# Rounding the sigmoids on GpSimd in the largest-output pass, and the key biases' product on 128 rows in the masked attention

## The chip, the cores and the metric

One core of a Trainium2 chip runs the whole program. The core has five engines that each work through their own list of instructions in order and wait for each other on semaphores: TensorE (matrix products, PE), VectorE (DVE), ScalarE (ACT), GpSimd (POOL) and SyncE (SP), which here only starts transfers. The metric is the device time of one execution in microseconds; lower is better. A profile is one more execution with every instruction recorded.

## The reference

Two decoder layers on x of shape (16, 256, 512): a cross attention, a quantized feed-forward network, a masked attention and a second feed-forward network with mixed low-rank parts, each added to x. The change touches two stages. The first is in the quantized network:

```python
up   = act_qdq(x @ lpbq_dequant(w_up).T)
gate = act_qdq(x @ lpbq_dequant(w_gate).T)
sig  = fixed_qdq_u16(jax.nn.sigmoid(gate))   # clip(round(sig * 65536), 0, 65535) / 65536
gate = act_qdq(gate * sig)
o    = act_qdq(gate * up)                    # its scale needs max |gate * up| over everything
return o @ lpbq_dequant(w_down).T
```

Since `act_qdq` divides by the largest magnitude of the whole tensor, the products have to be gone through once for the maximum before any of them can be used. The second is the masked attention:

```python
qp, kp = _proj(q, W1, b1, W2, b2), _proj(k, W1, b1, W2, b2)
qk   = einsum('bqd,bkd->bqk', qp, kp) / sqrt(512) + mask
return einsum('bqk,bkd->bqd', softmax(qk), v1)
```

The kernel folds both projections into the keys, so that a score is a product of normalized x with a folded key, plus one number for each key, the key bias.

## The kernel before

The stages run one after the other. **The largest-output pass** (`output_maximum`, names `om_`) cuts the 4096 x 1536 gates into 48 parts of 128x1024 that stay in SBUF as integers (`qf_gate`). Two parts make a pair. For an even part n the sigmoids are made here: ScalarE computes them into `sig` (L1614), VectorE rounds them to uint16 in `sq[:, 0, :]` (L1703); for an odd part they come rounded from HBM (`sq_d`, L1579), where the pass before left them. Then for each part: VectorE multiplies gate by sigmoid (`prod`, L1713), ScalarE scales the raw up-product (L1621, loaded by SP at L1582) and the product (L1623, back into `qf_gate`), VectorE multiplies both (`outp`, L1725) and reduces the magnitudes to a maximum (L1729). VectorE's order is written out: ahead of an even part's output product it rounds the sigmoids of the part after the next, n + 2; after each output product comes the sigmoid product of part n + 2, and then the reduction. `sig` is a single buffer, so the next sigmoid waits for `sq_done`; the next rounding waits for `prod_done`, since `sq[:, 0]` is single too.

Beside that pass, the keys of the masked attention are folded. TensorE turns the weights, multiplies them and forms a Gram matrix; from part 16 on it multiplies the Gram matrix with the context, eight chunks of 512 keys in four row blocks each, and forms the key biases. For that, half-chunks of the context are loaded by GpSimd (L1760, one buffer, so each load waits until TensorE has turned the last one), turned by TensorE (L1798) and split into a high part by ScalarE (L1632) and a low part by VectorE (L1718, one operand in PSUM). GpSimd also does the small tasks of the fold: it sets two tiles, loads context half 1, adds and spreads the key shift (L1770, L1772), splits the four Gram rows (L1775, L1777), forms and splits the shift's parts (L1779 to L1784), and then starts the other 14 context loads, in this order and each as soon as its wait is met. At the end it reduces the maximum over the partitions (L1788).

**The masked attention** (`masked_attention`, names `ma_`) goes through 16 batches of 256 tokens in a software pipeline. In step s TensorE turns x of batch s + 1 (L2256), forms the scores of batch s, turns the probabilities of s - 1 (L2281) and multiplies those of s - 2 with the values. The scores of each of two query tiles begin with the key biases: `ones[:]` of 2 rows times `trow[:, b, :]`, 2 rows by 256 keys (a high and a low part of the bias), at L2269, start=True; twelve products of 128 rows with 256 columns follow in the same PSUM tile (L190 to L192 in `product`). `trow` is loaded by SP (L2075) from `split_d` in HBM. GpSimd's list begins with a memset of `ones` (L2109), then come the deviations (L2097, L2099) and the low parts of keys and values (L2103, L2107).

Of the kernel before, what the change touches and what calls it, by code (L numbers as in the profile page):

```python
# [14 lines left out]
ALU = mybir.AluOpType  # L15
# [8 lines left out]
P = 128  # L24
# [1470 lines left out]
def output_maximum(nc, a, ctx_in, keys_d, bias_d, raw_up, gate, sq_d, big, scal, folds, wd, wd_parts, wd_late, ident):  # L1495
# [9 lines left out]
    with Phase(nc, "om") as ph:  # L1505
# [7 lines left out]
        mx_row = ph.sb("mx_row", [P, 1])  # L1513
        raw_ready = [ph.sem(f"raw_ready{i}") for i in range(2)]
        sq_ready = [ph.sem(f"sq_ready{i}") for i in range(2)]
        sig_ready, sq_done = ph.sem("sig_ready"), ph.sem("sq_done")
        up_ready, prod_done, gate_ready, out_done, max_done = (
            ph.sem(n) for n in ("up_ready", "prod_done", "gate_ready", "out_done", "max_done"))
        spacer = ph.sem("spacer")
# [46 lines left out]
        with nc.Block() as block:  # L1566
# [129 lines left out]

            @block.vector
            def _(dve):
                def rounded(n):
                    dve.wait_ge(sig_ready, n // 2 + 1)  # L1700
                    if n >= 2:
                        dve.wait_ge(prod_done, n - 1)
                    dve.tensor_scalar(sq[:, 0, :], sig[:], SIGQ, SIGQ - 1, ALU.mult, ALU.min).then_inc(sq_done, 1)  # L1703

                def products(n):
                    s = n % 2
                    if s:
                        dve.wait_ge(sq_ready[n // 2 % 2], 16 * (n // 4) + 16)
                    else:
                        dve.wait_ge(sq_done, n // 2 + 1)  # L1710
                    if n >= 2:
                        dve.wait_ge(gate_ready, n - 1)
                    dve.tensor_tensor(prod[:, s, :], place(n), sq[:, place_of(n), :], ALU.mult).then_inc(prod_done, 1)  # L1713

                def context_low(x):
                    c, lo = x // 2, x % 2 * S
                    dve.wait_ge(c_hi, x + 1)
                    dve.tensor_tensor(cT[c % 2][:, 1, :, lo:lo + S], ctp[:], cT[c % 2][:, 0, :, lo:lo + S].bitcast(F32), ALU.subtract).then_inc(c_low, 1)  # L1718

                def outputs(n):  # L1720
                    dve.wait_ge(gate_ready, n + 1)
                    dve.wait_ge(up_ready, n + 1)
                    if n:
                        dve.wait_ge(max_done, n)
                    dve.tensor_tensor(outp[:], place(n), up[:, n % 2, :], ALU.mult).then_inc(out_done, 1)  # L1725

                def largest(n):
                    dve.wait_ge(out_done, n + 1)
                    dve.tensor_reduce(mx[:, n:n + 1], outp[:], AX_X, ALU.max, apply_absolute_value=True).then_inc(max_done, 1)  # L1729

                rounded(0)
                products(0)
                products(1)
                for n in range(N):
                    if n % 2 == 0 and n + 2 < N:
                        rounded(n + 2)
                    outputs(n)
                    if n + 2 < N:
                        products(n + 2)
                    if n == 10:  # L1740
                        context_low(0)
                    if n == 15:
                        context_low(1)
# [12 lines left out]
            def _(pool):  # L1756
                def load_context(x):
                    if x:
                        pool.wait_ge(c_full, x)
                    pool.dma_start(cin[:], ctx_in[x * S:(x + 1) * S, :].rearrange("(t p) d -> p t d", p=P)).then_inc(c_ready, 16)  # L1760
# [3 lines left out]
                pool.wait_ge(cleared, 1)  # L1764
                pool.memset(gbraw, 1.0).then_inc(cleared, 1)
                pool.wait_ge(cleared, 2)
                load_context(1)
                pool.wait_ge(b_ready, 32)
                pool.wait_ge(beta_out, 1)
                pool.tensor_tensor(beta[:], bsum[:], b12[:, 1, :], ALU.add).then_inc(beta_ready, 1)  # L1770
                pool.wait_ge(beta_ready, 1)
                pool.tensor_tensor(betas, betas, beta[:].unsqueeze(2).broadcast_to([P, KD, P]), ALU.mult).then_inc(betas_ready, 1)  # L1772
                for d in range(KD):
                    pool.wait_ge(g_out, d + 1)
                    pool.tensor_copy(gram[:, 0, d, :], graw[:, d, :]).then_inc(gram_hi, 1)  # L1775
                    pool.wait_ge(gram_hi, d + 1)
                    pool.tensor_tensor(gram[:, 1, d, :], graw[:, d, :], gram[:, 0, d, :].bitcast(F32), ALU.subtract).then_inc(gram_low, 1)  # L1777
                pool.wait_ge(gc_out, 2)
                pool.tensor_tensor(gbraw, gbraw, gcol[:].unsqueeze(2).broadcast_to([P, KD, P]), ALU.mult).then_inc(gbraw_done, 1)  # L1779
                pool.wait_ge(gbraw_done, 1)  # L1780
                pool.wait_ge(turned, KD)
                pool.tensor_copy(gb[:, 0], gbraw).then_inc(gb_hi, 1)
                pool.wait_ge(gb_hi, 1)
                pool.tensor_tensor(gb[:, 1], gbraw, gb[:, 0].bitcast(F32), ALU.subtract).then_inc(gb_low, 1)  # L1784
                for x in range(2, 2 * NCH):
                    load_context(x)
                pool.wait_ge(row_max, 1)
                pool.partition_all_reduce(big[:, 0:1], mx_row[:], P, RMAX).then_inc(all_max, 1)  # L1788

# [195 lines left out]
def masked_attention(nc, a, ctx_in, keys_d, bias_d, split_d, x2, x3, sides, ident, neghalf):  # L1985
# [8 lines left out]
    with Phase(nc, "ma") as ph:  # L1994
# [13 lines left out]
        mask = ph.sb("mask", [P, NK, S])  # L2008
        traw = ph.sb("traw", [B, S])
        tsplit = ph.sb("tsplit", [B, 2, S], F32R)  # L2010
        trow = ph.sb("trow", [2, B, S], F32R)
        ones = ph.sb("ones", [2, P], F32R)
        logit = ph.sb("logit", [P, 2, NK, S])
        nm = ph.sb("nm", [P, 2, NK])
        prob = ph.sb("prob", [P, 2, NK, S])
# [7 lines left out]
        po = ph.ps("po", [P, NK, D])  # L2023
        x_ready, stored = ([ph.sem(f"{n}{i}") for i in range(NX)] for n in ("x_ready", "stored"))
        r_ready, c_ready = [ph.sem(f"r_ready{i}") for i in range(NR)], [ph.sem(f"c_ready{i}") for i in range(NC)]
        m_ready, traw_ready, t_high, t_low, t_stored, t_ready, ones_made = (
            ph.sem(n) for n in ("m_ready", "traw_ready", "t_high", "t_low", "t_stored", "t_ready", "ones_made"))
        stat_done, mv_ready, var_ready, rstd_ready, shift_ready, xn_ready, spacer_d, spacer_p, spacer_a = (
            ph.sem(n) for n in ("stat_done", "mv_ready", "var_ready", "rstd_ready", "shift_ready", "xn_ready", "spacer_d", "spacer_p", "spacer_a"))
        x_full, x_high, x_low, r_high, r_low, v_high, v_low = (  # L2030
# [10 lines left out]
        def _(sp):  # L2041
# [30 lines left out]
            load_keys(2)  # L2072
            load_x(3)
            sp.wait_ge(t_stored, 16)
            sp.dma_start(trow[:].bitcast(F32), split_d.rearrange("b a s -> a b s")).then_inc(t_ready, 16)  # L2075
            for s in range(LAST + 1):
                if s + 3 < B:
                    load_keys(s + 3)
# [13 lines left out]
        def _(pool):  # L2092
# [12 lines left out]
            def values_low(b):  # L2105
                pool.wait_ge(v_high, b + 1)
                pool.tensor_tensor(val[:, b % NB_, 1], cin[:, b % NC], val[:, b % NB_, 0].bitcast(F32), ALU.subtract).then_inc(v_low, 1)  # L2107

            pool.memset(ones[:].bitcast(F32), 1.0).then_inc(ones_made, 1)  # L2109
            for s in range(FIRST, B):  # L2110
                if 0 <= s + 2 < B:
# [752 lines left out]
```

## Time and profile before

| | us |
|---|---|
| median of 3 runs | 3375.27 (3375.1 to 3377.76) |
| the profiled execution, its own time | 3377.16 |
| its span | 3375.4 |
| PE busy | 3161.2 (94%) |
| DVE busy | 1962.9 (58%) |
| ACT busy | 1667.3 (49%) |
| POOL busy | 789.5 (23%) |

Busy time is over the whole span, in which stages with different limits follow each other; the largest-output pass lies between 1812 and 2036 us, the masked attention between 2318 and 2473. In the rows below a matmul's own length is modelled, since matmuls overlap: the step from one start to the next is what TensorE needed. VectorE's and ScalarE's instructions overlap a little too.

### The profile page before, as it was taken

Reading aid. Unit: us, or ns where it says so; the run is one execution under the profiler, and the core shown is the slowest. Engines: PE = TensorE matmul, PEld = TensorE weight load, DVE = VectorE, ACT = ScalarE, POOL = GpSimd, SP = SyncE. Lnnn points to the kernel's source line nnn. Section 1 sums busy time; section 2 is a strip of 40 time slices with the busy share of each in tenths; the row PEclk is TensorE's granted clock in tenths of the full one; section 3 lists DMA queues with packets and bytes.
Section 4 is the critical chain, followed back from the end, with each engine's and each line's share of the span. In section 5 each row is a group of like instructions: output and inputs, shape, how many; then the busy total and the mean of one; then the engine's idle time right before and its main releaser. Section 6 shows DMA issues by size and latency. Waiting matters only on the chain. (4 is left out here: it accounts for less than half of the span.)

```text
span 3375.4 us, 51188 instructions
## 1 busy us (share of the span) xinstructions
PE 3161.2 (94%) x16792; PEld 2696.3 (80%) x16792; DVE 1962.9 (58%) x3422; ACT 1667.3 (49%) x3204; POOL 789.5 (23%) x881
## 2 busy tenths in 40 slices
PE   7999979999999969999996798997979999999998
PEld 6988969999999958887884576885857888888886
DVE  3245549999999955557888995554752222222211
ACT  3132249999999943336776785564721111111110
POOL 0000038888888830000000200003700000000000
PEclk9999989999999989999997898998989999999999
DMA  6487755555555545556666686444831110001000
GB/s 187 120 253 228 224 171 165 170 177 173 170 165 173 157 150 198 179 172 203 226 218 219 215 265 218 158 161 165 251 116 60 38 35 24 31 26 38 32 25 13
DMA packets 370165, 503.46 MB, mean 149 GB/s; under 512 B 58940, under 2 KB 237420, under 8 KB 366032
## 3 DMA queue, kind: packets, MB, share of 16 engines
q1 hardware_dynamic: 356458, 473.37, 44.6%
q0 software_dynamic: 4768, 18.88, 1.7%
q10 hardware_dynamic: 8720, 8.41, 0.7%
q8 instruction: 124, 2.03, 0.3%
q14 instruction: 95, 0.78, 0.1%
HBM read 292.86 MB, written 174.11 MB: 138 GB/s over the span
## 5 line engine op out<-in xcount | busy, mean ns | idle before, releaser
L2592 DVE SCALAR_TENSOR_TENSOR lf_hT<-lf_hb,lf_hT 128x512 fp32r<-128x512 f32 x128 | 88.5, 691 | 571.6 <-ACT lf_hT L2668 571.6
L2668 ACT ACTIVATE lf_hT<-lf_hb 128x512 fp32r<-128x512 f32 x128 | 76.5, 598 | 669.2 <-PE lf_py L192 639.6
L768 POOL TENSOR_TENSOR at_prob<-at_prob,at_rec 128x308 f32<-128x308 f32 (+1 forms) x256 | 261.3, 1042 | 87.6 <-DVE at_rec L808 87.3
L908 ACT ACTIVATE at_prob<-at_sc,at_nm 128x77 f32<-128x77 f32 (+1 forms) x1024 | 277.6, 385 | 7.3 <-DVE at_nm L795 4.9
L190 PE MATMUL lf_hb<-lf_xT,lf_w 128*128 128x512 f32 x512 | 204.7, 400 | 1.3 <-DVE lf_hT L2592 1.3
L192 PE MATMUL lf_hb<-lf_xT,lf_w 128*128 128x512 f32 x512 | 203.5, 398 | 0.0
L190 PE MATMUL lf_py<-lf_w,lf_hT 128*128 128x512 f32 x512 | 203.1, 397 | 0.0
L192 PE MATMUL lf_py<-lf_w,lf_hT 128*128 128x512 f32 x512 | 203.1, 397 | 0.0
L191 PE MATMUL lf_hb<-lf_xT,lf_w 128*128 128x512 f32 x512 | 203.0, 396 | 0.0
L191 PE MATMUL lf_py<-lf_w,lf_hT 128*128 128x512 f32 x512 | 202.6, 396 | 0.0
L801 DVE TENSOR_REDUCE at_sums<-at_prob 128x4 f32<-128x308 f32 (+1 forms) x256 | 166.1, 676 | 17.7 <-ACT at_prob L908 17.5
L2521 POOL TENSOR_SCALAR lf_var<-lf_mv 128x1 f32<-128x1 f32 x32 | 7.3, 229 | 717.4 <-DVE lf_mv L2544 717.4
L190 PE MATMUL at_qb<-at_xT,xo_Wq 128*128 128x256 f32 x512 | 151.5, 296 | 23.4 <-DVE at_qst L825 12.0
L755 POOL TENSOR_TENSOR at_ks<-at_kr,at_ks 128x512 fp32r<-128x512 f32 x128 | 165.5, 1293 | 13.2 <-ACT at_ks L915 13.2
L190 PE MATMUL pg_bank<-qu_xs,qg_wg 128*128 128x512 f32 x384 | 153.0, 398 | 16.6 <-DVE qu_xs L1417 16.6
L190 PE MATMUL dn_py<-qf_wd,dn_om 128*128 128x512 f32 x384 | 150.7, 392 | 16.0 <-DVE dn_om L1938 16.0
L795 DVE TENSOR_REDUCE at_nm<-at_sc 128x4 f32<-128x308 f32 (+1 forms) x256 | 159.6, 665 | 6.3 <-PE at_sc L984 6.3
L812 DVE TENSOR_TENSOR at_pT<-at_tp,at_pT 128x1024 fp32r<-128x1024 f32 x128 | 156.3, 1221 | 3.3 <-ACT at_pT L921 0.3
L190 PE MATMUL pu_bank<-qu_xs,qu_wu 128*128 128x512 f32 x384 | 151.2, 394 | 7.1 <-SPq L1291 5.6
L1007 PE MATMUL at_sc<-at_pT,at_vs 128*128 128x256 f32 x1024 | 153.1, 292 | 1.4 <-issue 1.4
L191 PE MATMUL pg_bank<-qu_xs,qg_wg 128*128 128x512 f32 x384 | 150.6, 392 | 0.0
L191 PE MATMUL pu_bank<-qu_xs,qu_wu 128*128 128x512 f32 x384 | 150.6, 392 | 0.0
(334 smaller groups left out, 9229.3 us busy)
## 6 DMA issues: line engine op xcount, KB each, us to landing
at_kr<-k_rows SPq DMA_DIRECT2D x256, 128.0 KB, 2.9
at_qs<-at_qst SPq DMA_DIRECT2D x512, 64.0 KB, 2.0
raw_gate<-pg_stage SPq DMA_DIRECT2D x96, 256.0 KB, 2.0
pu_rg<-raw_gate SPq DMA_DIRECT2D x96, 256.0 KB, 3.2
raw_up<-pu_stage SPq DMA_DIRECT2D x96, 256.0 KB, 2.1
om_raw<-raw_up SPq DMA_DIRECT2D x48, 512.0 KB, 4.5
dn_raw<-raw_up SPq DMA_DIRECT2D x48, 512.0 KB, 3.8
xn_parts<-pr_xturned SPq DMA_DIRECT2D x32, 512.0 KB, 5.0
```

Of the source, the lines that this page charges most:

```text
L190: pe.matmul(out, lh, rh, start=start, stop=False, **kw)
L191: pe.matmul(out, lh, rl, start=False, stop=False, **kw)
L192: return pe.matmul(out, ll, rh, start=False, stop=stop, **kw)
L755: pool.tensor_tensor(ks[:, n % NK, :, 1, :], kr[:, n % NKR], ks[:, n % NK, :, 0, :].bitcast(F32), ALU.subtract).then_inc(k_low, 1)
L768: ins = pool.tensor_tensor(prob[:, i, :, lo:hi], prob[:, i, :, lo:hi], rec[:, z, g, :].unsqueeze(2).broadcast_to([P, 2 * NTE, hi - lo]), A ...
L795: ins = dve.tensor_reduce(nm[:, n % 2, g, :], sc[n % 2][:, :, lo:hi], AX_X, ALU.max, negate=True)
L801: dve.tensor_reduce(sums[:, z, g, :], prob[:, i, :, SEG[g][0]:SEG[g][1]], AX_X, ALU.add).then_inc(sum_done, 1)
L812: dve.tensor_tensor(pT[:, n % 2, 1], tp[:], pT[:, n % 2, 0].bitcast(F32), ALU.subtract).then_inc(pt_done, 1)
L908: ins = act.activation(prob[:, i, m, lo:hi], sc[n % 2][:, m, lo:hi], ACT.Exp, bias=nm[:, n % 2, g, m:m + 1])
L1007: ins = pe.matmul(attended(s)[:, h, :], vs[:, n % NVP, k, h, :, :].rearrange("p a d -> p (a d)"), pT[:, n % 2, part, k, h * S:(h + 1) * S] ...
L2592: dve.scalar_tensor_tensor(hT[:, i, 1, :], hb[i][:], 0.0, hT[:, i, 0, :].bitcast(F32), ALU.max, ALU.subtract).then_inc(h_done, 1)
L2668: act.activation(hT[:, m % 2, 0, :], hb[m % 2][:], ACT.Relu).then_inc(h_hi, 1)
```

## The change

In the largest-output pass the 24 roundings leave VectorE's list. GpSimd does each in two passes over 128x1024: `sig * 65536 + MAGIC` in place, with MAGIC = 12582912, which makes the sum a whole number, then `min(sig - MAGIC, 65535)` into the uint16 tile. A new semaphore `sig_whole` stands between them. GpSimd's other tasks keep their order among each other, but are now put in at given part numbers between the roundings. In the masked attention `ones` and `trow` get 128 rows; all rows of `trow` are cleared by GpSimd first, SP's load fills rows 0 and 1 and waits for that.

```diff
 @block.vector   # output_maximum
-                def rounded(n):
-                    dve.wait_ge(sig_ready, n // 2 + 1)
-                    if n >= 2:
-                        dve.wait_ge(prod_done, n - 1)
-                    dve.tensor_scalar(sq[:, 0, :], sig[:], SIGQ, SIGQ - 1, ALU.mult, ALU.min).then_inc(sq_done, 1)
...
-                rounded(0)
                 products(0)
                 products(1)
                 for n in range(N):
-                    if n % 2 == 0 and n + 2 < N:
-                        rounded(n + 2)
                     outputs(n)
...
 @block.gpsimd
+                def rounded(n):
+                    pool.wait_ge(sig_ready, n // 2 + 1)
+                    if n >= 2:
+                        pool.wait_ge(prod_done, n - 1)
+                    pool.tensor_scalar(sig[:], sig[:], SIGQ, MAGIC, ALU.mult, ALU.add).then_inc(sig_whole, 1)
+                    pool.wait_ge(sig_whole, n // 2 + 1)
+                    pool.tensor_scalar(sq[:, 0, :], sig[:], MAGIC, SIGQ - 1, ALU.subtract, ALU.min).then_inc(sq_done, 1)
...
+                rounded(0)
+                for n in range(N):
+                    if n == 10:
+                        load_context(1)
+                        key_shift()
+                    if 11 <= n < 11 + KD:
+                        gram_parts(n - 11)
+                    if n == 11 + KD:
+                        shift_parts()
+                    if n % 2 and 2 <= (n - 9) // 2 < 2 * NCH:
+                        load_context((n - 9) // 2)
+                    if n % 2 == 0 and n + 2 < N:
+                        rounded(n + 2)
...
 # masked_attention
-        trow = ph.sb("trow", [2, B, S], F32R)
-        ones = ph.sb("ones", [2, P], F32R)
+        trow = ph.sb("trow", [P, B, S], F32R)
+        ones = ph.sb("ones", [P, P], F32R)
...
             sp.wait_ge(t_stored, 16)
-            sp.dma_start(trow[:].bitcast(F32), split_d.rearrange("b a s -> a b s")).then_inc(t_ready, 16)
+            sp.wait_ge(trow_cleared, 1)
+            sp.dma_start(trow[0:2].bitcast(F32), split_d.rearrange("b a s -> a b s")).then_inc(t_ready, 16)
...
+            pool.memset(trow[:].rearrange("p b s -> p (b s)").bitcast(F32), 0.0).then_inc(trow_cleared, 1)
             pool.memset(ones[:].bitcast(F32), 1.0).then_inc(ones_made, 1)
```

GpSimd at the beginning of the largest-output pass, before (an ISA row is an instruction without operands, here one that goes ahead of another kind of work):

```order
L1760 DMA om_cin<-in_ctx_dram 128x2x512
L1763 MEMSET om_rout 128x512
L1765 MEMSET om_rout 128x512
L1760 DMA om_cin<-in_ctx_dram 128x2x512
L1770 ISA
L1770 TENSOR_TENSOR om_beta<-om_bsum,om_b 128x4
L1772 TENSOR_TENSOR om_rout<-om_rout,om_beta 128x512
L1775 CAST om_gram<-qf_fold 128x512
L1777 TENSOR_TENSOR om_gram<-qf_fold,om_gram 128x512
```

The same place now:

```order
L1751 DMA om_cin<-in_ctx_dram 128x2x512
L1754 MEMSET om_rout 128x512
L1756 MEMSET om_rout 128x512
L1763 ISA
L1763 TENSOR_SCALAR om_sig<-om_sig 128x1024
L1765 TENSOR_SCALAR om_sq<-om_sig 128x1024
L1763 TENSOR_SCALAR om_sig<-om_sig 128x1024
L1765 TENSOR_SCALAR om_sq<-om_sig 128x1024
```

The ISA row has moved from the key shift, behind the second context load, to the first rounding, behind the memsets. VectorE at the beginning of its loop, before:

```order
L1703 TENSOR_SCALAR om_sq<-om_sig 128x1024
L1713 TENSOR_TENSOR om_prod<-qf_gate,om_sq 128x1024 x2
L1703 TENSOR_SCALAR om_sq<-om_sig 128x1024
L1725 TENSOR_TENSOR om_outp<-qf_gate,om_up 128x1024
L1713 TENSOR_TENSOR om_prod<-qf_gate,om_sq 128x1024
L1729 TENSOR_REDUCE om_mx<-om_outp 128x1
L1725 TENSOR_TENSOR om_outp<-qf_gate,om_up 128x1024
L1713 TENSOR_TENSOR om_prod<-qf_gate,om_sq 128x1024
L1729 TENSOR_REDUCE om_mx<-om_outp 128x1
L1703 TENSOR_SCALAR om_sq<-om_sig 128x1024
```

VectorE now:

```order
L1707 TENSOR_TENSOR om_prod<-qf_gate,om_sq 128x1024 x2
L1719 TENSOR_TENSOR om_outp<-qf_gate,om_up 128x1024
L1707 TENSOR_TENSOR om_prod<-qf_gate,om_sq 128x1024
L1723 TENSOR_REDUCE om_mx<-om_outp 128x1
L1719 TENSOR_TENSOR om_outp<-qf_gate,om_up 128x1024
L1707 TENSOR_TENSOR om_prod<-qf_gate,om_sq 128x1024
```

Two products and a reduction follow each other without a rounding between the pairs. GpSimd at the beginning of the masked attention now:

```order
L2125 MEMSET ma_trow 128x4096
L2126 MEMSET ma_ones 128x128
L2113 TENSOR_TENSOR ma_rstd<-ma_var,neghalf 128x2
L2115 TENSOR_TENSOR ma_shift<-ma_minus,ma_rstd 128x2
L2119 TENSOR_TENSOR ma_rT<-ma_rraw,ma_rT 128x1024
```

The first row is new there, and the second had 2x128 elements.

## Rows read from the trace of the kernel before

**Rows 1.** Windows: stretch, length, each engine's busy us (instructions), PE clock, DMA share, GB/s.

```profile
1824.80:1892.70 67.90, 45.29 (x160) 26.78 (x161) 66.83 (x60) 49.07 (x55) 20.02 (x15) 0.73 0.55 169
1892.70:2034.50 141.80, 127.26 (x586) 102.72 (x584) 132.91 (x124) 118.88 (x132) 9.40 (x13) 0.98 0.82 269
2349.50:2462.40 112.90, 112.84 (x696) 96.33 (x696) 77.90 (x197) 78.44 (x137) 72.70 (x51) 0.98 0.70 219
```

**Rows 2.** Timeline of VectorE, first parts: start, length, line, operation, [idle before].

```profile
1825.36 1.22 DVE L1725 TENSOR_TENSOR om_outp<-qf_gate,om_up 128x1024 f32<-128x1024 int16 x1
...
1827.63 1.21 DVE L1729 TENSOR_REDUCE om_mx<-om_outp 128x1 f32<-128x1024 f32 x1
1828.98 1.23 DVE L1725 TENSOR_TENSOR om_outp<-qf_gate,om_up 128x1024 f32<-128x1024 int16 x1
...
1832.98 1.22 DVE L1725 TENSOR_TENSOR om_outp<-qf_gate,om_up 128x1024 f32<-128x1024 int16 x1
```

**Rows 3.** Timelines of GpSimd and VectorE beside the Gram parts, parts 12 and 13.

```profile
1866.67 0.61 POOL L1775 CAST om_gram<-qf_fold 128x512 fp32r<-128x512 f32 x1
...
1869.63 1.63 DVE L1713 TENSOR_TENSOR om_prod<-qf_gate,om_sq 128x1024 f32<-128x1024 int16 x1
...
1874.45 2.30 DVE L1713 TENSOR_TENSOR om_prod<-qf_gate,om_sq 128x1024 f32<-128x1024 int16 x1
```

**Rows 4.** GpSimd's groups, shapes apart: count, busy us, mean ns, idle before.

```profile
L2107 POOL TENSOR_TENSOR ma_val<-ma_cin,ma_val 128x1024 fp32r<-128x1024 f32 x16 | 38.4, 2399 | 3.2 <-ACT ma_val L2211 3.2
...
L2334 POOL MEMSET lo_ra<- 128x1024 f32 x1 | 1.0, 967 | 0.0
```

**Rows 5.** Waits of GpSimd: waited for, us, times, longest.

```profile
POOL dn_one L1895 <- issue: 12.1, 1, 12.1
POOL om_beta L1770 <- issue: 8.1, 1, 8.1
```

**Rows 6.** Timelines of GpSimd and ScalarE at the start of the largest-output pass.

```profile
1816.47 0.52 POOL L1765 MEMSET om_rout<- 128x512 f32 x1
...
1815.87 1.15 ACT L1621 ACTIVATE om_up<-om_raw,scal 128x1024 int16<-128x1024 f32 x1 [0.79 <-DMA om_raw<-raw_up]
```

**Rows 7.** Timelines of VectorE and GpSimd around parts 30 and 31.

```profile
1963.00 1.22 DVE L1718 TENSOR_TENSOR qf_wd<-om_ctp,qf_wd 128x1024 fp32r<-128x1024 f32 x1
...
1965.47 1.23 DVE L1725 TENSOR_TENSOR om_outp<-qf_gate,om_up 128x1024 f32<-128x1024 int16 x1
...
1966.16 0.72 POOL L1760 DMA_DIRECT2D om_cin<-in_ctx_dram  x1 [8.47 <-PE om_ctp L1798]
```

**Rows 8.** Timeline of TensorE, one batch of the masked attention.

```profile
2382.98 1.03 PE L2256 MATMUL ma_xtp<-ident,ma_xn 128*128 128x128 f32 x8
2383.95 0.38 PE L2269 MATMUL ma_sc<-ma_trow,ma_ones 2*128 2x256 f32 x1
2384.26 0.39 PE L190 MATMUL ma_sc<-ma_rT,ma_xT 128*128 128x256 f32 x1
2384.48 0.28 PE L191 MATMUL ma_sc<-ma_rT,ma_xT 128*128 128x256 f32 x1
2384.60 0.28 PE L192 MATMUL ma_sc<-ma_rT,ma_xT 128*128 128x256 f32 x1
...
2385.66 0.28 PE L192 MATMUL ma_sc<-ma_rT,ma_xT 128*128 128x256 f32 x1
2385.87 0.38 PE L2269 MATMUL ma_sc<-ma_trow,ma_ones 2*128 2x256 f32 x1
```

**Rows 9.** Timeline of TensorE, transposes ahead of 128-row products in the largest-output pass.

```profile
1964.82 1.03 PE L1798 MATMUL om_ctp<-ident,om_cin 128*128 128x128 f32 x8
1965.61 0.48 PE L190 MATMUL om_rb<-qf_wd,om_gram 128*128 128x512 f32 x1
```

**Rows 10.** Timelines of TensorE and GpSimd, early in the masked attention.

```profile
2349.55 1.57 PE L2256 MATMUL ma_xtp<-ident,ma_xn 128*128 128x128 f32 x8 [2.45 <-ACT ma_xn L2192]
...
2325.64 0.73 POOL L2097 TENSOR_TENSOR ma_rstd<-ma_var,neghalf 128x2 f32<-128x2 f32 x1 [4.95 <-DVE ma_var L2136]
```

More of the change, by code:

```diff
@@ L1515, in output_maximum @@
         sq_ready = [ph.sem(f"sq_ready{i}") for i in range(2)]
-        sig_ready, sq_done = ph.sem("sig_ready"), ph.sem("sq_done")
+        sig_ready, sig_whole, sq_done = ph.sem("sig_ready"), ph.sem("sig_whole"), ph.sem("sq_done")
         up_ready, prod_done, gate_ready, out_done, max_done = (
@@ L1766, in _, with key_shift, gram_parts @@
                 pool.wait_ge(cleared, 2)
[L1767 to L1773, printed above, removed]
+                def rounded(n):
[5 more added lines that the diff above has]
+                    pool.tensor_scalar(sq[:, 0, :], sig[:], MAGIC, SIGQ - 1, ALU.subtract, ALU.min).then_inc(sq_done, 1)
+                def key_shift():
+                    pool.wait_ge(b_ready, 32)
+                    pool.wait_ge(beta_out, 1)
+                    pool.tensor_tensor(beta[:], bsum[:], b12[:, 1, :], ALU.add).then_inc(beta_ready, 1)
+                    pool.wait_ge(beta_ready, 1)
+                    pool.tensor_tensor(betas, betas, beta[:].unsqueeze(2).broadcast_to([P, KD, P]), ALU.mult).then_inc(betas_ready, 1)
+                def gram_parts(d):
                     pool.wait_ge(g_out, d + 1)
@@ L1777, in _, with shift_parts @@
                     pool.tensor_tensor(gram[:, 1, d, :], graw[:, d, :], gram[:, 0, d, :].bitcast(F32), ALU.subtract).then_inc(gram_low, 1)
[L1778 to L1786, printed above, removed]
+                def shift_parts():
+                    pool.wait_ge(gc_out, 2)
+                    pool.tensor_tensor(gbraw, gbraw, gcol[:].unsqueeze(2).broadcast_to([P, KD, P]), ALU.mult).then_inc(gbraw_done, 1)
+                    pool.wait_ge(gbraw_done, 1)
+                    pool.wait_ge(turned, KD)
+                    pool.tensor_copy(gb[:, 0], gbraw).then_inc(gb_hi, 1)
+                    pool.wait_ge(gb_hi, 1)
+                    pool.tensor_tensor(gb[:, 1], gbraw, gb[:, 0].bitcast(F32), ALU.subtract).then_inc(gb_low, 1)
+                rounded(0)
[11 more added lines that the diff above has]
+                        rounded(n + 2)
                 pool.wait_ge(row_max, 1)
@@ L2025, in masked_attention @@
         r_ready, c_ready = [ph.sem(f"r_ready{i}") for i in range(NR)], [ph.sem(f"c_ready{i}") for i in range(NC)]
-        m_ready, traw_ready, t_high, t_low, t_stored, t_ready, ones_made = (
-            ph.sem(n) for n in ("m_ready", "traw_ready", "t_high", "t_low", "t_stored", "t_ready", "ones_made"))
+        m_ready, traw_ready, t_high, t_low, t_stored, t_ready, ones_made, trow_cleared = (
+            ph.sem(n) for n in ("m_ready", "traw_ready", "t_high", "t_low", "t_stored", "t_ready", "ones_made", "trow_cleared"))
         stat_done, mv_ready, var_ready, rstd_ready, shift_ready, xn_ready, spacer_d, spacer_p, spacer_a = (
```

## The prediction

> **What bounds the kernel now.** The change touches two stages, so I read the busy time by stretch first. In the largest-output pass VectorE works 66.83 of 67.90 us and then 132.91 of 141.80; ScalarE and GpSimd have room, TensorE is at 127.26 in the second stretch [rows 1]. VectorE is what must be shortened there. In the masked attention TensorE works 112.84 of 112.90 us, the other engines at most 78.44 [rows 1]: there only TensorE's order counts. The chain of waits names no line of either stage, so I went on to the timelines. In VectorE's, the step from one part's output product to the next is 3.62 us (1825.36 to 1828.98) where no rounding stands between, and 4.00 (to 1832.98) where one does [rows 2]. So a rounding costs VectorE 0.38 us, less than its own length: without it the output product waits longer for the reduction's signal, 1.35 us from the reduction's start (1827.63 to 1828.98) [rows 2]. In TensorE's timeline the reader is to see the starts around the two-row product: the products of the same size on 128 rows follow each other at 0.12 us, but it is followed after 0.31 and the next after 0.22 [rows 8].
>
> **Roundings leave VectorE.** 24 are removed. The first two lie ahead of the loop or in the wait for the first loads, and go into the term on the start below. 22 x 0.38 = **8.4 us saved**, as long as VectorE stays the bound.
>
> **Two passes on GpSimd for each.** The trace has no such pass: one input, two operations, 128x1024. The nearest rows: a cast of half that width took 0.61 us [rows 3], a memset of the full width 0.967 [rows 4], a two-input operation of the full width 2.399 [rows 4]. Twice the cast less its fixed part gives about 1.1, and I take that, since the memset shows the one-operand rate; 2.4 is the upper end. So 24 x 2.2 = 53 us on an engine with 9.40 of 141.80 us of work in the second stretch [rows 1]. It needs no more than it has.
>
> What counts is what GpSimd's reading does to VectorE. Beside a 512-wide cast VectorE's product (two operands in SBUF) took 1.63 us, beside a two-input operation 2.30, against 1.22 alone [rows 2, 3]: the two engines took turns, and VectorE lost 0.41 and 1.08. A pass twice as wide as the cast would cost 2 x 0.41, say 0.85 us, when a two-operand VectorE instruction stands behind it, and nothing beside the reduction or the context's low part (one operand in PSUM). Of each part, output product and sigmoid product are exposed; the 1.35 us from the reduction's start on are not. One pass of 1.1 fits beneath it, the second lands on a product. So for the 8 roundings of parts 4 to 18: 8 x 0.85 = 6.8. For the 14 of parts 20 to 46 there is a context part beside the reduction, a free stretch from 1963.00 to 1965.47, 2.47 us, into which two passes fit only if they start at once [rows 7]. GpSimd now has the context load ahead of the rounding in its queue; it was issued at 1966.16, when TensorE had turned the last block, after that stretch [rows 7]. A rounding queued behind it starts beside the next part's products. I take 0.5 us for each of these, 7.0; the ends are 0 and 1.7 (both passes exposed). Together **13.8 us lost**, between 0 and some 45 (passes at the two-input price: 2.16 held by each).
>
> The Trainium skill, GPSIMD Engine Reference, section "Elementwise - side-by-side cycle accounting", gives 1.03 cycles an element for loops of up to two operations and about 1.8 as the best general loop, 769 ns for 512 elements. The cast row is below that second figure. As an estimate from that page, 1.8 cycles would make a pass about 1.54 us, which is inside the first rival below.
>
> **The start of the pass.** GpSimd's first general arithmetic after a partition reduction waited 8.1 us in this pass, and 12.1 at the next stage, for nothing but its own issue [rows 5]. Before, that stood at the key bias, where nobody waited. The order now has it ahead of the first rounding, behind the memset that ends at 1816.99 [rows 6]. So rounding 0 ends at 1817.0 + 8.1 to 12.1 + 2.3 = 1827.4 to 1831.4. Behind it: ScalarE's sigmoid 2, scaled up-part 0 and scaled gate 0 (1.15 us each, a little overlapped [rows 6]), with VectorE's product 0 beside them, 3.3 us to output product 0: 1830.7 to 1834.7 against 1825.36 [rows 2]. **5.3 to 9.3 us later, 7.2 taken.** In this stretch VectorE has a microsecond of idle time [rows 1], so nothing gives it back. The load of up-part 2 waits for up-part 0 too, and shifts with it.
>
> **GpSimd's other tasks by part number.** Key shift, Gram parts and shift parts are the same instructions in the same order; they contend with the same products as before. Cost 0, with 3 us either way for three more or fewer stalls of 1.08. The later context loads pass into the queue behind roundings, with a whole pair of parts until TensorE wants them.
>
> **Key-bias product on 128 rows.** 32 products stay 32; the other 126 rows are zeros. From the eight transposes' start to the first product's start is 0.97 us (2382.98 to 2383.95), then 0.31 and 0.22, 1.50 up to 2384.48 [rows 8]. Where 128-row products follow the transposes, their eight took 0.79 (1964.82 to 1965.61) [rows 9]; then 0.12 twice, and I allow 0.08 for the change of kind behind the transposes: 1.11. Saved 0.39. The second of a batch: 0.21 (2385.66 to 2385.87) and again 0.31 and 0.22 [rows 8], 0.74 against 3 x 0.12 = 0.36; saved 0.38. From 2349.55 TensorE has no further wait to 2462.4 [rows 1, 10]: batches 2 to 15. 14 x 0.77 = **10.8 us saved**; ends 8 and 12. Next late would be ScalarE, 78.44 us in 102 left, so TensorE stays the bound. The new memset, four times 0.967 at most 3.9 us plus 0.2 for the ones, lies in the 4.95 us in which GpSimd waited for VectorE's first variance [rows 4, 10]; without that cover it would cost its length. SP's load of the biases waits for it, issued later than it ends.
>
> **Sum.** -8.4 + 13.8 + 7.2 - 10.8 = +1.8 us. The profiled execution took 3377.16 (span 3375.4), 1.9 above the median of 3375.27; on the median the sum is **3377**.
>
> **Rivals.**
> *Slower: the pass on GpSimd is dear.* For it: two operations and a conversion to uint16, which no row shows; against it the cast and the memset. At 1.75 us, midway between 1.1 and 2.4, each pass holds VectorE up for some 1.5: 8 x 1.85 + 14 x 1.6 = 37 instead of 13.8, so +25 and **3400**. It decides from a pass of about 1.25 us on, where each rounding loses 0.22 more and the sum passes +6.8.
> *Faster: both passes slip beneath the reduction and the context part.* For it: the free stretches of 1.35 and 2.47 us, and ScalarE no longer held by a rounding; against it the stalls in [rows 3] and the context load ahead. No stalls: -8.4 + 7.2 - 10.8 = -12, **3363**.
> *The padded product brings nothing:* the gaps around it belong to accumulating onto a fresh bank, not to two rows. Against it: the 128-row products behind transposes in [rows 9]. Then -8.4 + 13.8 + 7.2 = +12.6, **3388**.
> The Trainium skill, TensorE: Matmul & The Clock Gate, section "Why this matters for your kernels", says that a single product on 32 rows takes the time of one on 128. By that rule alone this last rival holds; the rows' 0.31 and 0.22 beside 0.12 differ from it, so I leave it its small chance.
>
> **How the numbers follow.** Forecast 0.50 (its own range 3371 to 3383, by the ends of the start, of the padded products and of the Gram parts, which are not all met at once), dear pass 0.28, free passes 0.11, no gain from padding 0.11. A measurement tells apart about 0.2%, 6.8 us. The forecast lies within it but for a few hundredths on both sides; the dear pass and the last rival are slower, the free passes faster: faster 0.12, same 0.48, slower 0.40. The range 3366 to 3402 leaves out the free passes and the dearer half of the first rival's upper tail, some 2 in 10.
>
> **What would show it.** VectorE's timeline: steps of 3.62 without a stall, and products of 2.0 to 2.1 us where GpSimd holds them, one in each pair of parts. GpSimd's groups: passes of 1.0 to 1.2 us; 1.25 or more and the first rival holds. The start: output product 0 at 1831 to 1835 and a wait for "issue" ahead of the first pass. TensorE: 0.12 instead of 0.31 and 0.22 around the bias product, and batches shorter by 0.77 us. I am wrong if ScalarE or a transfer takes up what TensorE gives back, or if GpSimd's first pass needs no such wait.

## The result, and the profile after

The changed kernel takes **3406.82 us** (median of 4 runs, 3404.77 to 3407.83) against 3375.47 for the kernel before on the same chip: a ratio of 1.0091, interval 1.0073 to 1.0108. That is 31 us more, where 1.8 more was forecast, and outside the range. The profiled execution took 3406.28 us, with a span of 3404.5.

The page first, busy time of the engines over the span:

```profile
PE 3152.6 (93%) x16792; PEld 2697.4 (79%) x16792; DVE 1967.9 (58%) x3398; ACT 1668.9 (49%) x3204; POOL 924.5 (27%) x930
```

GpSimd has 135 us more work than before. GpSimd's groups in the trace of after (count, busy us, mean ns, idle before) say what it is:

```profile
L1765 POOL TENSOR_SCALAR om_sq<-om_sig 128x1024 uint16<-128x1024 f32 x24 | 101.7, 4238 | 2.0
L1763 POOL TENSOR_SCALAR om_sig<-om_sig 128x1024 f32<-128x1024 f32 x24 | 28.1, 1170 | 25.8 <-issue 9.9 <-DVE om_prod L1707 9.6 <-ACT om_sig L1614 5.8
```

The first pass (L1763) costs what the cast of [rows 3] and the memset of [rows 4] promised. The second (L1765), over the same number of elements, takes 4.2 us, above even the two-input price of 2.399 in [rows 4].

**Where the time went by stage.** I measure the largest-output pass from the end of the partition reduction ahead of it to the start of the one that closes it. Before this is 224.95 us, 15.62 of them up to output product 0. After it is 265.39 (1807.77 to 2073.16), 25.24 of them up to output product 0: 40.4 more, 9.6 at the start and 30.8 behind it. The rest of the program gives back some 10.

The start, GpSimd's and VectorE's timelines of after (start, length, engine, line, operation, [idle before <- releaser]):

```profile
1824.92 1.04 POOL L1763 TENSOR_SCALAR om_sig<-om_sig 128x1024 f32<-128x1024 f32 x1 [9.88 <-issue]
1826.04 3.68 POOL L1765 TENSOR_SCALAR om_sq<-om_sig 128x1024 uint16<-128x1024 f32 x1
...
1833.01 1.23 DVE L1719 TENSOR_TENSOR om_outp<-qf_gate,om_up 128x1024 f32<-128x1024 int16 x1 [0.90 <-ACT qf_gate L1623]
```

The wait for issue is there, 9.88 us between the 8.1 and 12.1 of [rows 5], and 3.68 is the second pass with nothing of VectorE beside it. Next, both engines in the first parts:

```profile
1839.13 1.05 POOL L1763 TENSOR_SCALAR om_sig<-om_sig 128x1024 f32<-128x1024 f32 x1 [1.42 <-DVE om_prod L1707]
1840.27 4.69 POOL L1765 TENSOR_SCALAR om_sq<-om_sig 128x1024 uint16<-128x1024 f32 x1
...
1840.24 1.23 DVE L1719 TENSOR_TENSOR om_outp<-qf_gate,om_up 128x1024 f32<-128x1024 int16 x1
1841.38 2.06 DVE L1707 TENSOR_TENSOR om_prod<-qf_gate,om_sq 128x1024 f32<-128x1024 int16 x1
...
1848.33 1.23 DVE L1719 TENSOR_TENSOR om_outp<-qf_gate,om_up 128x1024 f32<-128x1024 int16 x1
```

From one output product to the next but one (a pair of parts) it is 8.09 us (1840.24 to 1848.33); [rows 2] gave 3.62 + 4.00 = 7.62. That is one product of 2.06 instead of 1.22 in each pair, as forecast. The second pass loses 1 us to the output product that runs when it begins, but the product behind is held for 0.84 us, not for the 3.7 that the pass needs. The same engines around parts 25 to 28, where the folding runs beside:

```profile
1963.75 0.77 POOL L1751 DMA_DIRECT2D om_cin<-in_ctx_dram  x1 [4.09 <-PE om_ctp L1813]
1964.57 1.06 POOL L1763 TENSOR_SCALAR om_sig<-om_sig 128x1024 f32<-128x1024 f32 x1
1965.71 4.49 POOL L1765 TENSOR_SCALAR om_sq<-om_sig 128x1024 uint16<-128x1024 f32 x1
...
1964.46 2.25 DVE L1707 TENSOR_TENSOR om_prod<-qf_gate,om_sq 128x1024 f32<-128x1024 int16 x1
...
1967.97 1.23 DVE L1719 TENSOR_TENSOR om_outp<-qf_gate,om_up 128x1024 f32<-128x1024 int16 x1
1970.23 1.22 DVE L1707 TENSOR_TENSOR om_prod<-qf_gate,om_sq 128x1024 f32<-128x1024 int16 x1 [1.03 <-POOL om_sq L1765]
```

Here the rounding stands behind the context load, which waits for TensorE. The pass ends at 1970.20, and the sigmoid product of part 28 waits 1.03 us for it. A pair of parts 17 to 39, from one odd output product to the next, takes 10.35 to 10.77 us. In the trace of before most took 8.75, from 1965.47 [rows 7] to this line:

```profile
1974.22 1.23 DVE L1725 TENSOR_TENSOR om_outp<-qf_gate,om_up 128x1024 f32<-128x1024 int16 x1
```

The pieces nearly add up: 8.75 - 0.38 for the rounding that left + 0.84 for a product held up + 1.03 of waiting = 10.24. The waits of after in the stretch 1900 to 2074 (us, times, longest) sum this up:

```profile
DVE om_prod L1707 <- POOL om_sq L1765: 19.5, 14, 3.5
```

**The masked attention.** TensorE's timeline of one batch in after, to be held against [rows 8], and GpSimd's at its beginning:

```profile
2411.46 1.03 PE L2273 MATMUL ma_xtp<-ident,ma_xn 128*128 128x128 f32 x8
2412.25 0.36 PE L2286 MATMUL ma_sc<-ma_trow,ma_ones 128*128 128x256 f32 x1
...
2412.57 0.28 PE L191 MATMUL ma_sc<-ma_rT,ma_xT 128*128 128x256 f32 x1
...
2413.76 0.28 PE L192 MATMUL ma_sc<-ma_rT,ma_xT 128*128 128x256 f32 x1
2413.89 0.28 PE L2286 MATMUL ma_sc<-ma_trow,ma_ones 128*128 128x256 f32 x1
2414.01 0.28 PE L190 MATMUL ma_sc<-ma_rT,ma_xT 128*128 128x256 f32 x1
2414.12 0.28 PE L191 MATMUL ma_sc<-ma_rT,ma_xT 128*128 128x256 f32 x1
...
2357.44 3.51 POOL L2125 MEMSET ma_trow<- 128x4096 f32 x1 [6.50 <-DMA x<-dn_y]
...
2363.09 0.73 POOL L2113 TENSOR_TENSOR ma_rstd<-ma_var,neghalf 128x2 f32<-128x2 f32 x1 [2.00 <-DVE ma_var L2153]
```

Transposes to the third product: 2411.46 to 2412.57, 1.11 us where 1.50 stood. Around the second bias product 0.13 + 0.12 + 0.11 = 0.36 where 0.74 stood. Both are what was forecast. The new memset is followed by a wait for VectorE, so the deviations behind it are not delayed.

### The profile page after: what moved, and what is told of

Read it like the earlier page. It is cut to its first block and busy times, and to the rows that moved or that the text cites. A ratio compares the mean times of both kernels' runs of the same rounds, so it can differ in the third digit from the quotient of the medians.

```text
span 3404.5 us, 51216 instructions
## 1 busy us (share of the span) xinstructions
PE 3152.6 (93%) x16792; PEld 2697.4 (79%) x16792; DVE 1967.9 (58%) x3398; ACT 1668.9 (49%) x3204; POOL 924.5 (27%) x930
## 5 line engine op out<-in xcount | busy, mean ns | idle before, releaser
L801 DVE TENSOR_REDUCE at_sums<-at_prob 128x4 f32<-128x308 f32 (+1 forms) x256 | 166.2, 676 | 17.9 <-ACT at_prob L908 17.7
```

The costliest lines, as they stand in the source:

```text
L801: dve.tensor_reduce(sums[:, z, g, :], prob[:, i, :, SEG[g][0]:SEG[g][1]], AX_X, ALU.add).then_inc(sum_done, 1)
```

## The experiments

My theory after this was: the price of the second pass is the whole error, and it reaches VectorE through `sq_done`, because the rounding stands late in GpSimd's list. The rival: the dear pass keeps VectorE from its second operand for its whole length. In the table, "start" and "behind" are the stage's lengths up to output product 0 and from there to the closing reduction, from the traces; "over before" compares medians on one chip (e7 is a single run).

| kernel | start | behind | over before, us |
|---|---|---|---|
| before | 15.62 | 209.33 | |
| changed | 25.24 | 240.15 | +31.4 |
| e1 padded product alone | 15.68 | 208.56 | -10.2 |
| e2 roundings alone | 25.18 | 241.96 | +42.9 |
| e4 early first operation | 16.03 | 238.23 | +18.7 |
| e5 cheap second pass | 23.05 | 217.65 | +6.7 |
| e6 rounding ahead of load | 25.69 | 244.12 | +35.9 |
| e7 an extra dear pass | 29.08 | 237.26 | +32.8 |
| e8 one pass | 15.62 | 204.91 | -15.9 |
| e9 loads on ScalarE | 25.75 | 221.70 | +16.0 |
| e10 padded product alone, again | 16.01 | 208.72 | -9.6 |
| e11 one pass, again | 16.16 | 205.15 | -11.2 |

### The two parts apart (e1, e2)

e1 is the kernel before with the masked attention's part of the diff, e2 the kernel before with the other part.

> Kernel before with the key-bias product on 128 rows alone. If the masked attention brings what its part of the sum said (14 batches x 0.77 us) and the rest of the program does not take it back: 9 to 11 us less than before, about 3365 us. If the 9.4 us that the trace of after gives back outside the largest-output pass come from something else (an earlier start of later stages, transfers): within 3 us of before.

> The changed kernel with the masked attention as before. If the two parts add up: the largest-output pass costs 38 to 42 us more than before, about 3415 us, and 9 to 11 us more than the whole change. If the loss partly belongs to the masked attention (its new memset, its later load): less than 36 us more than before.

Measured: e1 3367.67 against 3377.89, ratio 0.9970 (0.9958 to 0.9983); e2 3420.83, ratio 1.0127 (1.0111 to 1.0142). The sum, 42.9 - 10.2 = 32.7, is the whole change within what can be measured. The padded product does what was forecast, and its memset and later load cost nothing that shows. The loss lies in the roundings alone.

### What makes the second pass dear (e3)

```diff
-                    pool.tensor_scalar(sq[:, 0, :], sig[:], MAGIC, SIGQ - 1, ALU.subtract, ALU.min).then_inc(sq_done, 1)
+                    f = n // 2 % 8
+                    if f == 0:
+                        ins = pool.tensor_scalar(sq[:, 0, :], sig[:], MAGIC, SIGQ - 1, ALU.subtract, ALU.min)
+                    elif f == 1:
+                        ins = pool.tensor_scalar(sig[:], sig[:], MAGIC, SIGQ - 1, ALU.subtract, ALU.min)
...
+                    ins.then_inc(sq_done, 1)
```

> The changed kernel with eight forms of GpSimd's second pass in turn over the 24 roundings, so that most even parts get wrong or stale sigmoids. Theory 'the conversion to uint16 is dear': the forms that write f32 take 1.05 to 1.2 us alone, all that write uint16 take 3 us or more. Rival 'the min is dear': subtract and min into f32 takes about 3.6 us, a plain subtract into uint16 1.1 to 1.5. Rival 'the pair of subtract and min, as against mult and add': subtract alone and mult with min about 1.1, subtract with min 3.6 whatever it writes.

GpSimd's timeline of e3, the shortest execution of each form; L1767 and L1769 are subtract with min (into uint16, into f32), L1771 and L1773 subtract alone (the same), L1775 a multiply and an add into uint16, L1777 a cast into uint16, L1779 a multiply and a min into f32, L1781 a multiply and an add into f32:

```profile
1824.95 3.68 POOL L1767 TENSOR_SCALAR om_sq<-om_sig 128x1024 uint16<-128x1024 f32 x1
...
1910.35 3.63 POOL L1769 TENSOR_SCALAR om_sig<-om_sig 128x1024 f32<-128x1024 f32 x1
...
2001.19 2.77 POOL L1771 TENSOR_SCALAR om_sq<-om_sig 128x1024 uint16<-128x1024 f32 x1
...
2010.98 2.77 POOL L1773 TENSOR_SCALAR om_sig<-om_sig 128x1024 f32<-128x1024 f32 x1
...
1939.99 1.05 POOL L1775 TENSOR_SCALAR om_sq<-om_sig 128x1024 uint16<-128x1024 f32 x1
...
2030.34 1.03 POOL L1777 CAST om_sq<-om_sig 128x1024 uint16<-128x1024 f32 x1
...
2036.71 4.48 POOL L1779 TENSOR_SCALAR om_sig<-om_sig 128x1024 f32<-128x1024 f32 x1
...
2044.59 1.05 POOL L1781 TENSOR_SCALAR om_sig<-om_sig 128x1024 f32<-128x1024 f32 x1
```

The longer executions of a form hold time in which the pass waited for a VectorE product; so may all three of multiply with min (4.48 to 4.50). The total of e3, 3395.33 us in a single run, mixes the forms and is not used. So none of the three theories is right as put. The uint16 costs nothing. It is the operation: subtract is dear by itself, a min in the second place is dear beside a multiply too, multiply and add are cheap. `x - MAGIC` and `x * 1.0 + (-MAGIC)` are the same number at 2.77 and 1.05 us.

### The second pass at the forecast's price (e5)

```diff
-                    pool.tensor_scalar(sq[:, 0, :], sig[:], MAGIC, SIGQ - 1, ALU.subtract, ALU.min).then_inc(sq_done, 1)
+                    pool.tensor_scalar(sq[:, 0, :], sig[:], 1.0, -MAGIC, ALU.mult, ALU.add).then_inc(sq_done, 1)
```

> The changed kernel with the second pass written as sig * 1.0 + (-MAGIC), a multiply and an add as in the first pass; the clip at 65535 is left out. Theory 'the prediction failed at the price of the second pass and nowhere else': pass 2 takes 1.05 us alone, no product waits for the rounding, and the whole comes to what was predicted for it, 3371 to 3383 us. Rival 'the rounding is late in parts 20 to 46 because it stands behind the context load, whatever the pass costs': products still wait there and the whole stays above 3393 us.

Measured: 3384.96 against 3378.23, ratio 1.0020 (1.0011 to 1.0030). Of the 31 us some 25 are gone, and no product behind part 2 waits for a rounding. VectorE and GpSimd in e5, parts 20 to 46:

```profile
1951.43 1.89 POOL L1765 TENSOR_SCALAR om_sq<-om_sig 128x1024 uint16<-128x1024 f32 x1
...
1949.21 1.23 DVE L1719 TENSOR_TENSOR om_outp<-qf_gate,om_up 128x1024 f32<-128x1024 int16 x1
1950.35 2.06 DVE L1707 TENSOR_TENSOR om_prod<-qf_gate,om_sq 128x1024 f32<-128x1024 int16 x1
...
1958.43 1.22 DVE L1719 TENSOR_TENSOR om_outp<-qf_gate,om_up 128x1024 f32<-128x1024 int16 x1
```

A pair takes 9.22 us here, and 8.09 in the first parts, exactly what the dear pass gave there. So in the first parts the length of the second pass costs nothing but GpSimd's own time. What is left over the 1.8 us of the sum is 4.9 us. By the stage's lengths 2.9 of it lie behind the start (8.3 more than before, where -8.4 + 13.8 = 5.4 was forecast), 0.2 at it, and the other 1.8 outside the stage. The 2.9 go with stalls that were taken too low: in parts 20 to 46 ten of the 14 roundings hold a product up by 0.8 us or more, where 0.5 was taken for each.

### The way to VectorE (e6, e7, e9)

e6 puts each rounding ahead of the context load:

```diff
-                    if n % 2 and 2 <= (n - 9) // 2 < 2 * NCH:
-                        load_context((n - 9) // 2)
                     if n % 2 == 0 and n + 2 < N:
                         rounded(n + 2)
+                    if n % 2 == 0 and 2 <= (n - 10) // 2 < 2 * NCH:
+                        load_context((n - 10) // 2)
```

> The changed kernel, dear second pass and all, with each rounding put ahead of the context load in GpSimd's list in parts 14 to 46. Theory 'the dear pass costs VectorE time through sq_done, since it starts late behind the load': no product of parts 20 to 46 waits for the rounding, the pair of parts falls from about 10.5 to 9.0 to 9.5 us, the whole to 3384 to 3394 us. Rival 'the dear pass holds the port of VectorE for its whole length wherever it stands': the pair of parts stays at 10 us or more and the whole within 4 us of the changed kernel, 3403 to 3411 us.

Measured: 3414.17, ratio 1.0105 (1.0089 to 1.0122); not faster than the changed kernel. The time is the rival's, but the pairs are not: they alternate between 9.2 to 9.7 us and 11 to 14. TensorE, ScalarE and VectorE in e6 show why, behind a load that GpSimd issued only at the end of its second pass (at 1950.26):

```profile
1950.32 0.77 POOL L1751 DMA_DIRECT2D om_cin<-in_ctx_dram  x1
...
1959.15 1.97 PE L1813 MATMUL om_ctp<-ident,om_cin 128*128 128x128 f32 x8 [5.78 <-DMA om_cin<-in_ctx_dram]
...
1961.16 1.02 ACT L1632 ACTIVATE qf_wd<-om_ctp 128x1024 fp32r<-128x1024 f32 x1 [8.71 <-PE om_ctp L1813]
...
1964.29 1.22 DVE L1719 TENSOR_TENSOR om_outp<-qf_gate,om_up 128x1024 f32<-128x1024 int16 x1 [4.76 <-ACT qf_gate L1623]
```

The wait has changed its owner. The load is late now, TensorE turns late, ScalarE stands at the copy of the turned block with VectorE's gates queued behind it, and VectorE waits 4.76 us. So my theory was too narrow: two jobs in GpSimd's list, either of which makes the other late.

e7 has the cheap second pass, and behind it a dear one for nothing that only ScalarE's next sigmoid waits for:

```diff
...
+                    pool.wait_ge(sq_done, n // 2 + 1)
+                    pool.tensor_scalar(sig[:], sig[:], MAGIC, SIGQ - 1, ALU.subtract, ALU.min).then_inc(sig_free, 1)
...
```

> The kernel with the cheap second pass, and behind each rounding, after it has been signalled, one more pass of subtract and min over the same tile in place, for nothing; ScalarE's next sigmoid waits for it, with several us to spare. So 24 dear passes are back, but no product waits for them. Theory 'a dear pass costs VectorE at most one stall of about 0.85 us': 0 to 20 us more than with the cheap pass alone. Rival 'it holds the port for its length': 2.6 to 3.6 us for each of 22, 57 to 80 us more.

Measured: 3411.07 (one run), 26 us over e5: between the two. ScalarE did wait:

```profile
ACT om_sig L1614 <- POOL om_sig L1767: 70.7, 22, 22.4
```

so the several us to spare that I counted on were not there, and the total of e7 doesn't settle it. It excludes the 57 us of a port held throughout. Its rows say more: a dear pass begins at 1932.35, and the output product that starts 0.28 us later takes 1.84 us instead of 1.23, while the pass goes on to 1935.98.

```profile
1932.35 3.63 POOL L1767 TENSOR_SCALAR om_sig<-om_sig 128x1024 f32<-128x1024 f32 x1
...
1932.63 1.84 DVE L1719 TENSOR_TENSOR om_outp<-qf_gate,om_up 128x1024 f32<-128x1024 int16 x1
```

e9 is the changed kernel with the context loads taken out of GpSimd's list:

```diff
                     act.activation(cT[c % 2][:, 0, :, lo:lo + S], ctp[:], ACT.Copy).then_inc(c_hi, 1)
+                    if x + 1 < 2 * NCH:
+                        act.dma_start(cin[:], ctx_in[(x + 1) * S:(x + 2) * S, :].rearrange("(t p) d -> p t d", p=P)).then_inc(c_ready, 16)
...
```

> The changed kernel, dear second pass and all, with the context loads issued by ScalarE right behind its copy of the block before, so that nothing but the roundings and the small tasks is left in GpSimd's list. Theory 'the loss of parts 20 to 46 is two jobs in one queue, each late behind the other': no product waits for a rounding and no turn for a load, the pair of parts falls from about 10.4 to 9.2 to 9.7 us, the whole comes 8 to 18 us below the changed kernel, that is 13 to 23 us above the kernel before on the same chip. Rival 'the dear pass itself takes the time from VectorE or ScalarE': the pair stays above 10.2 us and the whole 28 us or more above the kernel before.

Measured: 3393.19 against 3377.17, +16.0, ratio 1.0053 (1.0039 to 1.0068). GpSimd and VectorE in e9:

```profile
1986.43 1.04 POOL L1765 TENSOR_SCALAR om_sig<-om_sig 128x1024 f32<-128x1024 f32 x1 [2.27 <-DVE om_prod L1710]
1987.56 3.63 POOL L1767 TENSOR_SCALAR om_sq<-om_sig 128x1024 uint16<-128x1024 f32 x1
...
1987.33 1.21 DVE L1726 TENSOR_REDUCE om_mx<-om_outp 128x1 f32<-128x1024 f32 x1
1988.67 1.23 DVE L1722 TENSOR_TENSOR om_outp<-qf_gate,om_up 128x1024 f32<-128x1024 int16 x1
1989.81 1.22 DVE L1710 TENSOR_TENSOR om_prod<-qf_gate,om_sq 128x1024 f32<-128x1024 int16 x1
...
1997.05 1.23 DVE L1722 TENSOR_TENSOR om_outp<-qf_gate,om_up 128x1024 f32<-128x1024 int16 x1
```

Most pairs take 8.38 (1988.67 to 1997.05) or 9.22 us. With the dear pass still in the kernel, VectorE's step is now often that of no stall at all (8.75 in the trace of before, less 0.38). Here the dear pass begins beneath the reduction, 1.11 us ahead of the first of the two products inside its 3.63 us, and slows neither. What the pass costs in parts 20 to 46 is thus shown to come from GpSimd's list, not from its length on VectorE's operands. What is left over stands at the start, in the first pair (11.7 us against 9.1 in e5) and in the pair of the Gram tasks (parts 14 to 16, 17.9 us against 13.3), where the small tasks queue behind the roundings.

### The start (e4)

```diff
 @block.vector
+                for n in (0, 2):
+                    rounded(n)
...
 @block.gpsimd
-                rounded(0)
+                pool.tensor_scalar(scrap[:], gbraw[:, 0, 0:1], 1.0, 0.0, ALU.mult, ALU.add)
```

`rounded` on VectorE is that of the kernel before.

> The changed kernel with the first two roundings on VectorE again, and a GpSimd operation of one column behind its second memset, so that the wait for issue is spent while nobody waits for GpSimd. If the late start of the pass is what the first rounding cost: output product 0 some 9.6 us earlier than in the changed kernel, about 1823.4 us by its clock, and the whole about 3397 to 3399 us. If the wait moves to the next GpSimd operation that counts (rounding of part 4), or the pass waits for something else there: within 3 us of the changed kernel, 3404 to 3408 us.

Measured: 3396.56, ratio 1.0058 (1.0043 to 1.0073), 18.7 us over the kernel before on its chip, where the changed kernel is 31.4 over it on its own: 12.7 less. Output product 0 at 1822.48, 16.03 us from the stage's start, where the changed kernel needs 25.24; behind it the first pair takes 8.3 us instead of 11.7, with the second rounding on VectorE again. The wait has not gone away, it lies where nobody waits:

```profile
1824.18 0.70 POOL L1799 TENSOR_SCALAR om_scrap<-om_rout 128x1 f32<-128x1 f32 x1 [10.48 <-issue]
```

### One cheap pass (e8, and e1 and e8 again side by side)

With the start of e4 and the order of e6, and, as in e5, without the clip at 65535:

```diff
-                    pool.tensor_scalar(sig[:], sig[:], SIGQ, MAGIC, ALU.mult, ALU.add).then_inc(sig_whole, 1)
-                    pool.wait_ge(sig_whole, n // 2 + 1)
-                    pool.tensor_scalar(sq[:, 0, :], sig[:], MAGIC, SIGQ - 1, ALU.subtract, ALU.min).then_inc(sq_done, 1)
+                    pool.tensor_scalar(sq[:, 0, :], sig[:], SIGQ, 0.0, ALU.mult, ALU.add).then_inc(sq_done, 1)
```

> The changed kernel with each rounding as a single GpSimd pass, sig * 65536 + 0 straight to uint16 (no clip at 65535, and the conversion has to round), put ahead of the context load, and the first two roundings on VectorE with GpSimd's first operation early. If a pass of 1.05 us lies beneath the reduction or the context part: no stalls, 8.4 us gained in the pass, 3357 to 3362 us, 6 to 10 less than the padded product alone (3367.67). If it lands on a product each time: 8.4 - 22 x 0.85 = -10.3, 3375 to 3380 us. Between: it breaks even with the padded product alone.

> The kernel before with the padded key-bias product alone, again, on the same chip as the next one: ratio to the kernel before 0.997, as in its first run.

> The single cheap GpSimd pass with the early start and the padded product, again, beside the padded product alone. If the roundings on GpSimd now gain what leaving VectorE was worth in parts 4 to 18 (8 x 0.38 = 3.0 us) and half of it behind: 3 to 7 us less than the padded product alone. If the two differ by chips only: within 2 us of it.

Measured: e8 3362.29, ratio 0.9960 (0.9946 to 0.9974). Side by side: the padded product alone 3367.54, ratio 0.9970 (0.9960 to 0.9980), one pass 3365.93, ratio 0.9966 (0.9954 to 0.9978). Both beat both kernels; they can't be told apart by total time. The traces do tell them apart: the stage takes 220.5 and 221.3 us with the single pass, 224.2 and 224.7 with the roundings on VectorE, 3.7 and 3.4 less. e8 in the first parts:

```profile
1840.26 1.05 POOL L1773 TENSOR_SCALAR om_sq<-om_sig 128x1024 uint16<-128x1024 f32 x1 [6.20 <-DVE om_prod L1714]
...
1837.75 1.22 DVE L1726 TENSOR_TENSOR om_outp<-qf_gate,om_up 128x1024 f32<-128x1024 int16 x1
...
1840.02 1.21 DVE L1730 TENSOR_REDUCE om_mx<-om_outp 128x1 f32<-128x1024 f32 x1
...
1844.99 1.23 DVE L1726 TENSOR_TENSOR om_outp<-qf_gate,om_up 128x1024 f32<-128x1024 int16 x1
```

One pass of 1.05 us lies beneath the reduction of 1.21; the pair takes 7.24 us, 0.38 less than before, with no stall. In parts 20 to 46 it gains little: pairs of 8.37 alternate with 8.7 to 8.84, where the pass meets an output product, for instance here:

```profile
1984.75 1.04 POOL L1773 TENSOR_SCALAR om_sq<-om_sig 128x1024 uint16<-128x1024 f32 x1 [6.44 <-ACT om_sig L1615]
...
1985.19 1.68 DVE L1726 TENSOR_TENSOR om_outp<-qf_gate,om_up 128x1024 f32<-128x1024 int16 x1
```

The Trainium skill, GPSIMD: programming the Q7 cores, section "SBUF Data Layout", says, for code on the cores and as measured with one way of setting the streams up, that the conversion on the way to SBUF rounds to the nearest and saturates. This form relies on that; no run here shows what it makes of a sigmoid at the upper end.

## Why the prediction was wrong

- **Two passes on GpSimd for each: the term that failed.** "Twice the cast less its fixed part gives about 1.1, and I take that ... 2.4 is the upper end." It held for the first pass (1.04 alone) and not for the second (3.63 to 3.68), which is above the upper end. The rows that I priced it by are a cast, a memset and a two-input operation; none has a subtract of an immediate or a min, and I let the tile's size and the count of operands stand for the operation. e3 shows that the operation decides, e5 that at 1.05 us the total is 6.7 over before. From this term come 22.5 us behind the start (240.15 - 217.65) and 2.2 at it. The waits of VectorE's products for a rounding, behind output product 0, fall from 24.1 us in all to 0.9 with the cheap pass, which is as much as the 22.5.
- **Stalls of VectorE (+13.8): the size was a little low.** 0.84 per pair in the first parts, as taken (0.85). In parts 20 to 46 of e5 mostly 0.84 too, not 0.5, since most roundings, behind the load, began beside a product, as the prediction feared. That the stall would grow with the length of the pass, as the first rival has it, did not come out: a pass of 3.63 us holds a product no longer than one of 1.05. (The upper end, put at some 45, is 22 x 2.16 = 47.5.)
- **"It needs no more than it has", GpSimd's room: wrong as a test.** Even with 130 us of passes GpSimd was busy for only 153 of the 240 us behind output product 0. What counted was when the passes ended. The prediction named the context load ahead of the rounding and priced only the stall that follows from it, not that the product itself waits for the rounding: 19.5 us in 14 waits.
- **Roundings leave VectorE (-8.4): right per step, 0.38 a pair** (7.24 against 7.62 in e8), but a pair keeps it only where no stall takes it back: 4.4 us of the 8.4 in e8 (204.91 against 209.33), and 3.6 against the padded product alone side by side (205.15 against 208.72).
- **The start (+7.2): right in its mechanism, and its check was met partly by luck.** The wait of 9.88 us for issue came where it was put. Output product 0 at 1833.01 lies within 1831 to 1835, but the whole stage began 2.0 us earlier than in the trace of before. Counted from the stage's start it came 9.6 us late, just above the end of 9.3, since the dear second pass lies on this way too; with the cheap pass (e5) it was 7.4. The term also stopped at output product 0: the product of part 2 then waited another 3.52 us for the second rounding, 0.94 in e5.
- **Padded product (-10.8): right.** 0.39 + 0.38 in the batch shown, as forecast, -10.2 and -9.6 us in all (e1, and again in e10).
- **The rivals.** The dear pass is what happened, by its condition and on its side, at 3407 instead of 3400, but by another mechanism: it was to hold VectorE up for some 1.5 us a pass, and it held it for 0.84 a pair and let it wait for its result. The Trainium skill, SBUF — State Buffer, section "SBUF: two separate sides", says that of a VectorE operation with two SBUF inputs and a GpSimd operation the first to start has the port for the whole instruction. The trace agrees for the wait of the pass itself (4.69 behind an output product, 3.68 without) and not for the product behind a dear pass: 0.84 us at 1841.38, 0.61 at 1932.63 in e7, nothing at 1967.97 nor at 1988.67 and 1989.81 in e9, all with the pass going on. The measurement decides. The free passes came true only with a single pass (e8) and there only in the first parts, and the rival that padding brings nothing fell.

## What to carry to other kernels

Price an instruction that no row shows by its operation, not by its size, and put the upper bound well above the nearest row; on GpSimd try a multiply and an add first, since the same number by a subtract cost 2.6 times as much here. When work moves to an engine with room, ask who waits for each result and what stands ahead of it in that engine's list: room over a stage says nothing about a result that comes 1 us late in every turn. A wait for issue after a change of the kind of work is cheapest bought early, with an operation that nobody needs.

## What the runs showed of the hardware

- GpSimd, one input of 128x1024 f32: multiply with add 1.05 us, into f32 or uint16; cast into uint16 1.03; subtract alone 2.77; subtract with min 3.63 to 3.68; multiply with min 4.48 to 4.50 in all of three. Subtract with min took 4.47 to 4.49 where it began beside a VectorE product, so multiply with min may well be 3.6 by itself; that is an estimate.
- A GpSimd pass held a VectorE product of two SBUF operands up until about 0.9 us after the pass's own start, however long the pass was. The dear pass of e7 began 0.28 ahead of a product and held it 0.61 (1932.35); the single pass of e8 began 0.44 ahead of one and held it 0.45 (1984.75); a dear pass that began 0.89 (1914.22 in the trace of after) or 1.11 us ahead (e9) held nothing. The full stall of 0.84 is a pass that starts just ahead of the product. Some products behind a context load's issue lost more (2.25 us at 1964.46 in the trace of after); what held these was not taken apart.
- Why the hold ends there stays open. That the pass's operand reading lies at its front is how I read these rows; no run took it apart.
- The wait for issue ahead of GpSimd's first general arithmetic behind a partition reduction was 9.8 to 12.0 us where it stood at the first rounding or at the one-column operation (10.5 and 10.4 there, in e4 and e11), and 8.1 to 9.0 where it stood at the key bias, in before, e1 and e10.
